# Routed tiles of a mixture-of-experts stage: gated rows turned by SyncE's transposing DMAs instead of TensorE, down product two tiles later

## The chip, the cores and the metric

The kernel runs on one core of one Trainium2 chip. The metric is the device time of one launch. Names used below: TensorE (PE, the matmuls; PEld its weight loads), VectorE (DVE), ScalarE (ACT), GpSimd (POOL) and SyncE (SP), which here only issues DMAs, in the order of its program. The core has 16 DMA engines; SP's transfers go over the hardware queue, POOL's accumulating ones over the software queue.

## The reference, cut to what matters

x has shape (8, 256, 512) in float32. A long convolution over products of value and context rows comes first and is added to x; the change doesn't touch it. Then follows the feed-forward part over T = 2048 tokens of 512 numbers:

```python
scores = sigmoid(xf @ gate_w.T)                    # 8 experts
topk_w, topk_idx = top_k(scores, 2)
topk_w = topk_w / (topk_w.sum(-1, keepdims=True) + 1e-20) * 2.5
shared_out = silu(xf @ shared_wg.T) * (xf @ shared_wu.T) @ shared_wd.T
h = silu(xf @ exp_wg[e].T) * (xf @ exp_wu[e].T)    # for each expert e, 352 wide
all_out = h @ exp_wd[e].T
out = x + shared_out + sum over the two picked experts of topk_w * all_out
```

## The kernel before

**Precision.** Every float32 operand of a product is split into a high and a low fp16 part, and a product is three fp16 matmuls, high x high, high x low and low x high (split_products, L734 to L736). So wherever a result becomes an operand, ScalarE makes the high part (a copy to fp16) and VectorE the low part (a subtraction).

**Routed tiles.** The pairs of token and expert are sorted by expert in a buffer in DRAM (pair_rows, fp16 high and low parts side by side), in tiles of 128 pairs. There are TILES = 39 places for tiles, as many as any routing can need. A tile that isn't needed is computed all the same, on rows that are thrown away. For every tile t:

- SyncE loads its rows with a transposing DMA (load_tile, L525, eight blocks of 128x128) into one of four slots (xg), and its token numbers and weights (load_ids, L528).
- tile_gate_up on TensorE: 24 matmuls of 352 columns, 12 for gate into bank 0 and 12 for up into bank 1. The transposed rows are the stationary operand, so the result has tokens on partitions.
- ScalarE: silu of the gate (tile_silu, L1147). VectorE: silu times up into hm (tile_gated, L1535).
- tile_hidden on TensorE: the down product needs the hidden numbers on partitions, so three 128x128 transposes in float32 turn hm into bank 3 (L930). The third overlaps the second, since 352 isn't a multiple of 128; its rows that come twice meet weights that are zero.
- ScalarE copies bank 3 to fp16 (tile_hidden_high, L1159), VectorE subtracts (tile_hidden_low, L1540), both into mixT (hgh, hgl).
- tile_down on TensorE: 9 matmuls of 512 columns into bank 4. ScalarE scales the result by the pair's weight (tile_out, L1154), and POOL adds it to the rows of out with an indirect accumulating DMA (add_tile, L697).

**Order around the change.** All orders are written out by hand, one program for each engine, with semaphores between them. TensorE's loop is gate/up of t, down of t-1, transposes of t. The add of tile t waits for the add of t-2; where t begins another expert, or is a tile not needed, it waits for t-1 as well (tile_prev), since a token can occur in both. SyncE loads the rows of t+4 when gate/up of t has left their slot, and the ids of t+4 when the add of t has landed. Tile 0 is interleaved with the last down product of the shared part.

**Expert weights.** They are loaded raw, four pieces an expert, into staging buffers, and turned into fp16 parts by ScalarE (L1068) and VectorE (L1398). Expert 7 comes last: SyncE loads it behind the store of the last group of base rows (L401, out of x_tok), and its conversion is queued on ScalarE and VectorE between the work of tiles 1 and 2 (two pieces each). TensorE waits for all weights before it enters its loop at tile 5.

Of the kernel before, what the change touches and what calls it, by code (L numbers as in the profile page):

```python
# [5 lines left out]
ALU = mybir.AluOpType  # L6
# [7 lines left out]
P = 128  # L14
# [24 lines left out]
TILES = 2 * T // P + E - 1  # L39
EROWS = T + P  # L40
# [13 lines left out]
def xattn_moe(nc, x, ctx, ctx_hidden, skip, krev, gate_w, shared_w, expert_w, consts, table0, zeros, out):  # L54
# [8 lines left out]
    with ExitStack() as stack:  # L63
# [132 lines left out]
        hgh, hgl = (mixT[:, EX_PIECE + i * FK * P // 2:EX_PIECE + (i + 1) * FK * P // 2].bitcast(F16) for i in range(2))  # L196
# [22 lines left out]
        rows_in = [sem(f"rows_in{i}") for i in range(RING)]  # L219
        added = [sem(f"added{i}") for i in range(2)]  # L220
# [160 lines left out]
        def _(sp):  # L381
# [162 lines left out]
            for t in range(RING, 2 * RING):  # L544
                sp.wait_ge(r_gu, t - RING + 1)
                load_tile(t, t % RING)
                if t >= RING + 2:
                    sp.wait_ge(added[t % 2], 16)
                    load_ids(t - 2, t - 2 - RING)
            with sp.Fori(2, TILES // RING) as j:  # L550
                for u in range(RING):
                    t = j * RING + u
                    sp.wait_ge(r_gu, t - RING + 1)
                    sp.sem_inc(sp_passed, 1)
                    load_tile(t, u)
                    sp.wait_ge(added[u % 2], 16 * (j * (RING // 2) + (u - 2 - RING) // 2 + 1))
                    sp.sem_inc(sp_passed, 1)
                    load_ids(t - 2, (u + 2) % RING)
            for t in range(TILES // RING * RING, TILES + 2):
                if t < TILES:  # L560
                    sp.wait_ge(r_gu, t - RING + 1)
                    load_tile(t, t % RING)
                sp.wait_ge(added[t % 2], 16 * ((t - 2 - RING) // 2 + 1))
                load_ids(t - 2, (t - 2) % RING)
# [154 lines left out]
        def _(pe):  # L719
# [206 lines left out]
            def tile_hidden(t):  # L926
                pe.wait_ge(r_hm, t + 1)
                for k in range(FK):
                    c = min(k * P, FF - P)
                    last = nc.tensor.transpose(bank[3][:, k * P:(k + 1) * P], hm[:, c:c + P], ident)  # L930
                last.then_inc(r_hT, 1)

            def tile_down(t, w):
                pe.wait_ge(r_hl, t + 1)
                if not isinstance(t, int) or t > 0:
                    pe.wait_ge(r_y, t)
                last = split_products(
                    bank[4],
                    lambda k: (hgh[:, k * P:(k + 1) * P], hgl[:, k * P:(k + 1) * P]),
# [10 lines left out]
            tile_hidden(0)  # L950
            for t in range(1, RING + 1):
# [3 lines left out]
                if t == 1:  # L955
                    pe.wait_ge(base_ready, Q * (G - 1) + 1)
                tile_down(t - 1, weights_of(t - 1))
                if t < RING:
                    following = weights_of(t + 1), need_of(t + 1)
                tile_hidden(t)  # L960
            pe.wait_ge(piece_l, (E - 1) * EX_PARTS)
            with pe.Fori(1, (TILES - 3) // RING) as j:
                for u in range(1, RING + 1):
                    t = RING * j + u
                    tile_gate_up(t, u % RING, j + u // RING + 1, weights_of(t))
                    tile_down(t - 1, weights_of(t - 1))
                    tile_hidden(t)
            for t in range(TILES - 2, TILES):
                tile_gate_up(t, t % RING, t // RING + 1, weights_of(t))
                tile_down(t - 1, weights_of(t - 1))  # L970
                tile_hidden(t)
            tile_down(TILES - 1, weights_of(TILES - 1))
# [3 lines left out]
        def _(act):  # L976
# [180 lines left out]
            def tile_hidden_high(t):  # L1157
                act.wait_ge(r_hT, t + 1)
                nc.scalar.copy(hgh, bank[3][:, 0:FK * P]).then_inc(r_hh, 1)  # L1159

            tile_silu(0)
            tile_hidden_high(0)
# [465 lines left out]
```

## Time and profile before

| | before |
|---|---|
| median of 3 runs | 769.8 us (769.48 to 770.99) |
| the profiled execution | 771.41 us |
| its span, first to last instruction | 769.6 us |
| mean granted TensorE clock | 0.96 |
| busy | PE 679.9 us (88%), DVE 434.9, POOL 387.1, ACT 288.2 |
| DMA | 84.28 MB, 110 GB/s on the mean |
| hardware queue, software queue | 33.5% and 13.7% of 16 engines' span |

Busy times are shares of the whole span, over stages with different limits. The routed tiles take the last third of it, from 517.5 us on. A matmul's listed duration (0.31 or 0.38 us) overlaps the next one's; how fast they follow is read from their starts. A wait is put down to the event that came last.

### The profile page before, as it was taken

The page shows a single profiled execution, that of the slowest core. Times are in us where ns is not written, and L with a number is a line of the kernel's source. Part 1 is how long each engine was busy: PE and PEld are TensorE (multiplying, and loading weights), DVE is VectorE, ACT ScalarE, POOL GpSimd, SP SyncE. Part 2 cuts the span into 40 slices and gives each one's busy share as a digit, 9 for nine tenths or more (in the row PEclk, how much of TensorE's full clock was granted, in tenths as well). Part 3 has the DMA queues.
Part 4 walks back from the last instruction along what each step waited for, and adds up shares of the span by engine and source line. Part 5 has one row for each costly group of instructions (what it writes and reads, how often), then busy time and mean ns, then how long its engine had stood idle before and what let it go on. Part 6 is the DMA issues. An engine that isn't in the chain of part 4 may idle for free.

```text
span 769.6 us, 11432 instructions
## 1 busy us (share of the span) xinstructions
PE 679.9 (88%) x3552; PEld 343.8 (45%) x3553; DVE 434.9 (57%) x662; ACT 288.2 (37%) x362; POOL 387.1 (50%) x333
## 2 busy tenths in 40 slices
PE   1786977969989969989999988798999999999992
PEld 1333433424444434444444433334566666665661
DVE  4798689667975666877695685872311111111110
ACT  4436646444223534223531257452322222222220
POOL 2889988385782574783867107700222322222231
PEclk9998998989999989999999999989899999999998
DMA  7933223601334600314224288986765565656533
GB/s 206 270 89 95 88 78 68 151 6 23 131 76 100 147 14 29 123 29 81 58 68 156 78 252 291 316 174 171 113 94 93 85 89 90 94 82 93 91 50 41
DMA packets 101364, 84.28 MB, mean 110 GB/s; under 512 B 68064, under 2 KB 81888, under 8 KB 100768
## 3 DMA queue, kind: packets, MB, share of 16 engines
q1 hardware_dynamic: 92128, 65.16, 33.5%
q0 software_dynamic: 9200, 18.65, 13.7%
q8 instruction: 21, 0.34, 0.2%
q14 instruction: 15, 0.12, 0.1%
HBM read 44.35 MB, written 25.68 MB: 91 GB/s over the span
## 4 chain that ended last, share of the span: by engine, by line
PE 59%; DVE 14%; ACT 9%; POOL 8%; issue 5%; DMA 3%; SPq 1%; POOLq 0%; another core or an unknown queue 0%; DVEq 0%; ACTq 0%
PE banks L734 18%; PE banks L736 18%; PE banks L735 18%; POOL arena L584 5%; POOL arena L609 2%; DVE stats L1243 2%; DVE arena L1230 2%; DVE mixT L1237 2%; PE banks L756 2%; PE banks L930 2%; ACT arena L1068 2%; DVE arena L1216 1%; DMA arena<-split_filters 1%; DVE hm L1364 1%; DMA stages<-in_expert_w 1%
## 5 line engine op out<-in xcount | busy, mean ns | idle before, releaser
L584 POOL TENSOR_TENSOR arena<-arena 128x512 f32<-128x512 f32 x124 | 136.1, 1129 | 67.0 <-DVE arena L1216 65.7
L697 POOL DMA_INDIRECT out<-xf,ids x39 | 60.8, 1559 | 198.8 <-ACT xf L1154 95.6
L734 PE MATMUL banks<-arena 128*128 128x512 f16 x320 | 125.3, 392 | 19.6 <-DVE arena L1230 9.7
L735 PE MATMUL banks<-arena 128*128 128x512 f16 x320 | 125.3, 392 | 0.6 <-issue 0.6
L736 PE MATMUL banks<-arena 128*128 128x512 f16 x320 | 125.1, 391 | 0.0
L1230 DVE TENSOR_TENSOR arena<-banks,arena 128x512 f32<-128x512 f32 x128 | 81.5, 683 | 38.3 <-PE banks L736 37.9
L734 PE MATMUL banks<-arena,normed 128*128 x312 | 98.4, 315 | 0.4 <-issue 0.4
L735 PE MATMUL banks<-arena,normed 128*128 x312 | 98.3, 315 | 0.0
L736 PE MATMUL banks<-arena,normed 128*128 x312 | 98.2, 315 | 0.0
L989 ACT ACTIVATE arena<-arena 128x2048 f16<-128x2048 f32 x31 | 59.1, 1907 | 87.3 <-POOL arena L584 87.2
L609 POOL TENSOR_TENSOR arena<-arena 128x512 f16<-128x512 f32 x68 | 78.8, 1191 | 7.6 <-ACT arena L989 7.5
L1540 DVE TENSOR_TENSOR mixT<-banks,mixT 128x384 f16<-128x384 f32 x39 | 21.8, 558 | 99.5 <-ACT mixT L1159 99.5
L1154 ACT ACTIVATE xf<-banks,ids 128x512 f32<-128x512 f32 x39 | 26.8, 687 | 126.9 <-PE banks L736 124.0
L1237 DVE TENSOR_REDUCE mixT<-arena 128x256 f32<-128x2048 f32 x32 | 73.1, 2285 | 1.0
L734 PE MATMUL banks<-xf,arena 128*128 128x512 f16 x176 | 68.8, 391 | 2.8 <-DVE hm L1364 2.4
L735 PE MATMUL banks<-xf,arena 128*128 128x512 f16 x176 | 68.8, 391 | 0.0
L736 PE MATMUL banks<-xf,arena 128*128 128x512 f16 x176 | 68.6, 390 | 0.0
L1535 DVE SCALAR_TENSOR_TENSOR hm<-banks,silu 128x352 f32<-128x352 f32 x39 | 20.5, 525 | 82.5 <-PE banks L736 82.5
L982 ACT ACTIVATE arena<-arena 128x1024 f16<-128x1024 f16 x32 | 33.7, 1054 | 84.4 <-PE banks L736 71.7
L734 PEld LDWEIGHTS banks<-arena 128*128 128x128 f16 x320 | 32.1, 100 | 62.5 <-issue 20.2
L735 PEld LDWEIGHTS banks<-arena 128*128 128x128 f16 x320 | 32.1, 100 | 40.4 <-issue 7.0
L736 PEld LDWEIGHTS banks<-arena 128*128 128x128 f16 x320 | 32.1, 100 | 40.1 <-issue 4.6
(164 smaller groups left out, 1132.3 us busy)
## 6 DMA issues: line engine op xcount, KB each, us to landing
arena<-split_filters SPq DMA_DIRECT2D x32, 256.0 KB
arena<-in_expert_w SPq DMA_DIRECT2D x12, 544.0 KB, 8.2
stages<-in_expert_w SPq DMA_DIRECT2D x10, 544.0 KB, 6.2
arena<-in_ctx_hidden SPq DMA_DIRECT2D x4, 1024.0 KB, 8.1
arena<-in_ctx SPq DMA_DIRECT2D x8, 512.0 KB, 6.5
x_tok<-in_x SPq DMA_DIRECT2D x6, 512.0 KB, 7.4
out<-x_tok SPq DMA_DIRECT2D x6, 512.0 KB, 5.4
x_tok<-in_expert_w SPq DMA_DIRECT2D x5, 544.0 KB
```

Source lines behind the costliest of these rows:

```text
L584: nc.gpsimd.tensor_tensor(kv[s % 2][:, lb * COLS:(lb + 1) * COLS].rearrange("p (b j i) -> p b j i", i=NH, j=NH), v[:, a, None, :].to_broad ...
L609: nc.gpsimd.tensor_tensor(kvl[s % SPLITS][:, c], kv[s % 2][:, c], kvh[s % SPLITS][:, c], ALU.subtract).then_inc(kvl_by_pool, 1)
L697: nc.gpsimd.indirect_dma_start(out=out, out_offset=bass.IndirectOffsetOnAxis(ap=ids[slot][:, 0:1], axis=0), in_=yg[slot], in_offset=None, ...
L734: nc.tensor.matmul(dst, wh, xh, start=(k == 0), stop=False)
L735: nc.tensor.matmul(dst, wh, xl, start=False, stop=False)
L736: last = nc.tensor.matmul(dst, wl, xh, start=False, stop=(k == n - 1))
L982: nc.scalar.activation(filt[s % 2].rearrange("p (t l) -> p t l", t=2), back, ACT.Copy).then_inc(filt_ready, 1)
L989: nc.scalar.activation(kvh[s % SPLITS], kv[s % 2], ACT.Copy).then_inc(kvh_ready, 1)
L1154: nc.scalar.activation(yg[slot], bank[4], ACT.Copy, scale=ids[slot][:, 1:2].bitcast(F32)).then_inc(r_y, 1)
L1230: nc.vector.tensor_tensor(prod[:, n * COLS:(n + 1) * COLS].rearrange("p (b j i) -> p b j i", i=NH, j=NH), bank[n].rearrange("p (b j i) -> ...
L1237: nc.vector.tensor_reduce(heads(mixT)[:, :, h * NH:(h + 1) * NH], prod.rearrange("p (a j i) -> p a j i", i=NH, j=NH), AX_X, ALU.add).then_ ...
L1540: nc.vector.tensor_tensor(hgl, bank[3][:, 0:FK * P], hgh, ALU.subtract).then_inc(r_hl, 1)
```

## The change

What turns the gated rows is moved from TensorE to the DMA engines, for all tiles but the last two:

- VectorE writes the gated rows into hm in two pieces: 256 columns, and the last 96 behind 32 columns of zeros. hm then has three whole blocks, and needs no overlap.
- ScalarE and VectorE split hm itself, token by token (tile_high, tile_low), into by_token, two slots in x_tok[1].
- SyncE turns both parts with one transposing DMA of six 128x128 blocks into by_hidden, two slots in mixT (turn_hidden), when the low part is there and the down product of t-2 has left the slot.
- TensorE's loop is gate/up of t, down of t-2. The down product waits for the DMA (hidden_in). gate/up of t waits for the gated rows of t-1 (r_hm), which the transposes did before.
- The last two tiles (TURNED_LAST) are transposed on TensorE as before, and both down products follow behind all else.
- On SyncE, expert 7's loads come right after the first ids, ahead of the store of the base rows, which now follows tile 0's turned rows. On ScalarE and VectorE its conversion comes at tiles 2 and 3 instead of 1 and 2.

The core of the diff:

```diff
+TURNED_LAST = 2
...
-        hgh, hgl = (mixT[:, EX_PIECE + i * FK * P // 2:EX_PIECE + (i + 1) * FK * P // 2].bitcast(F16) for i in range(2))
+        by_token, by_hidden = ([t[:, EX_PIECE + i * FK * P:EX_PIECE + (i + 1) * FK * P].bitcast(F16) for i in range(2)]
+                               for t in (x_tok[1].rearrange("p q l -> p (q l)"), mixT))
+        whole = (FK - 1) * P
+        hm_tail = slice(FK * P - FF + whole, FK * P)
...
-            sp.wait_ge(base_ready, Q * G)
-            store(out_rows[G - 1], x_tok[(G - 1) % 3], base_stored)
             load_expert(E - 1)
...
+            def turn_hidden(t, slot):
+                if not isinstance(t, int) or t >= 2:
+                    sp.wait_ge(r_down, t - 1)
...
+                sp.wait_ge(r_hl, t + 1)
...
+                sp.dma_start(by_hidden[slot].rearrange("p (a t) -> p a t", t=P), by_token[slot], transpose=True
+                             ).then_inc(hidden_in[slot], 16)
+
+            for t in range(RING):
+                sp.wait_ge(r_gu, t + 1)
+                load_tile(t + RING, t)
+                turn_hidden(t, t % 2)
+                if t == 0:
+                    sp.wait_ge(base_ready, Q * G)
+                    store(out_rows[G - 1], x_tok[(G - 1) % 3], base_stored)
+            with sp.Fori(1, TILES // RING - 1) as j:
                 for u in range(RING):
-                    t = j * RING + u
-                    sp.wait_ge(r_gu, t - RING + 1)
+                    t = RING * j + u
+                    sp.wait_ge(r_gu, t + 1)
                     sp.sem_inc(sp_passed, 1)
-                    load_tile(t, u)
...
+                    load_tile(t + RING, u)
+                    turn_hidden(t, u % 2)
+                    sp.wait_ge(added[u % 2], 16 * (RING // 2 * j + u // 2 - 1))
...
             def tile_gate_up(t, slot, n, w):
                 pe.wait_ge(rows_in[slot], 16 * n)
+                if not isinstance(t, int) or t > 0:
+                    pe.wait_ge(r_hm, t)
...
                 for u in range(1, RING + 1):
                     t = RING * j + u
                     tile_gate_up(t, u % RING, j + u // RING + 1, weights_of(t))
-                    tile_down(t - 1, weights_of(t - 1))
-                    tile_hidden(t)
-            for t in range(TILES - 2, TILES):
+                    tile_down(t - 2, u % 2, RING // 2 * j + u // 2, weights_of(t - 2))
+            for t in range(TILES - TURNED_LAST, TILES):
                 tile_gate_up(t, t % RING, t // RING + 1, weights_of(t))
-                tile_down(t - 1, weights_of(t - 1))
+                tile_down(t - 2, t % 2, t // 2, weights_of(t - 2))
                 tile_hidden(t)
-            tile_down(TILES - 1, weights_of(TILES - 1))
+            for t in range(TILES - TURNED_LAST, TILES):
+                tile_down(t, t % 2, None, weights_of(t))
...
+            def tile_high(t, slot, n):
+                act.wait_ge(r_hm, t + 1)
+                if not isinstance(n, int) or n > 0:
+                    act.wait_ge(hidden_in[slot], 16 * n)
+                nc.scalar.copy(by_token[slot][:, 0:FK * P], hm[:, 0:FK * P]).then_inc(r_hh, 1)
...
             for t in range(1, RING + 1):
                 tile_silu(t)
-                tile_out(t - 1, (t - 1) % RING, (t - 1) // RING + 1)
-                tile_hidden_high(t)
-
-                if t <= 2:
-                    expert(E - 1, *(first_half, second_half)[t - 1])
+                tile_high(t, t % 2, t // 2)
+                if t >= 2:
+                    tile_out(t - 2, (t - 2) % RING, (t - 2) // RING + 1)
+                if 2 <= t <= 3:
+                    expert(E - 1, *(first_half, second_half)[t - 2])
...
             def tile_gated(t):
+                if not isinstance(t, int) or t > 0:
+                    dve.wait_ge(r_hl, t)
...
+                nc.vector.scalar_tensor_tensor(out=hm[:, 0:whole], in0=bank[1][:, 0:whole], scalar=1 / WS,
+                                               in1=silu[:, 0:whole], op0=ALU.mult, op1=ALU.mult)
+                nc.vector.scalar_tensor_tensor(out=hm[:, hm_tail], in0=bank[1][:, whole:FF], scalar=1 / WS,
+                                               in1=silu[:, whole:FF], op0=ALU.mult, op1=ALU.mult).then_inc(r_hm, 1)
+
+            def tile_low(t, slot):
+                dve.wait_ge(r_hm, t + 1)
                 dve.wait_ge(r_hh, t + 1)
-                nc.vector.tensor_tensor(hgl, bank[3][:, 0:FK * P], hgh, ALU.subtract).then_inc(r_hl, 1)
-
+                nc.vector.tensor_tensor(by_token[slot][:, FK * P:2 * FK * P], hm[:, 0:FK * P],
+                                        by_token[slot][:, 0:FK * P], ALU.subtract).then_inc(r_hl, 1)
```

The order of instructions shows three places. The first is TensorE's loop, between the last matmul of one tile's down product (from mixT) and the first of the next tile's gate/up (from normed, the slot's rows); L930 are the transposes. Before:

```order
L736 MATMUL banks<-arena,mixT 128x512
L927 REGISTER_ALU
L930 MATMUL banks<-con,hm 128x128 [waits r_hm]
L930 MATMUL banks<-con,hm 128x128 x2
L896 ISA
L896 TENSOR_LOAD tile_w
L896 ISA x2
L734 ISA [waits rows_in3]
L734 MATMUL banks<-arena,normed 128x352
```

After:

```order
L755 MATMUL banks<-arena,mixT 128x512
L915 ISA
L915 TENSOR_LOAD tile_w
L915 ISA x2
L753 ISA [waits r_hm,rows_in3]
L753 MATMUL banks<-arena,normed 128x352
```

The two rows of transposes are gone, and the wait for hm stands at the gate/up instead. The second place is one tile of SyncE's loop. Before:

```order
L522 ISA [waits r_gu]
L522 TENSOR_LOAD tile_row
L522 ISA x2
L525 ISA
L525 DMA_TRANSPOSE normed<-pair_rows 128x8x128
L556 ISA
L522 TENSOR_LOAD tile_row [waits added0]
L522 ISA x2
L528 ISA
L528 DMA ids<-pair_table 128x2
```

After:

```order
L527 ISA [waits r_gu]
L527 TENSOR_LOAD tile_row
L527 ISA x2
L530 ISA
L530 DMA_TRANSPOSE normed<-pair_rows 128x8x128
L556 DMA_TRANSPOSE mixT<-x_tok 128x6x128 [waits r_down,r_hl]
L573 REGISTER_ALU
L527 ISA [waits added0]
L527 TENSOR_LOAD tile_row
L527 ISA x2
L533 ISA
L533 DMA ids<-pair_table 128x2
```

Between the load of a tile's rows and its ids there is now the DMA that turns the split rows, with two waits, and the waits of the ids stand behind it. The third place is SyncE at the start of the routed tiles, from the last of the first four ids on. Before:

```order
L522 TENSOR_LOAD tile_row
L522 ISA x2
L528 ISA
L528 DMA ids<-pair_table 128x2
L401 DMA out<-x_tok 64x4x512 [waits base_ready]
L401 DMA out<-x_tok 64x4x512
L417 DMA stages<-in_expert_w 128x1088 [waits piece_l] x2
L417 DMA x_tok<-in_expert_w 128x1088 [waits piece_l]
L417 DMA mixT<-in_expert_w 128x1088 [waits piece_l]
L522 TENSOR_LOAD tile_row [waits r_gu]
L522 ISA x2
L525 ISA
L525 DMA_TRANSPOSE normed<-pair_rows 128x8x128
```

After:

```order
L527 TENSOR_LOAD tile_row
L527 ISA x2
L533 ISA
L533 DMA ids<-pair_table 128x2
L422 DMA stages<-in_expert_w 128x1088 [waits piece_l] x2
L422 DMA x_tok<-in_expert_w 128x1088 [waits piece_l]
L422 DMA mixT<-in_expert_w 128x1088 [waits piece_l]
L527 TENSOR_LOAD tile_row [waits r_gu]
L527 ISA x2
L530 ISA
L530 DMA_TRANSPOSE normed<-pair_rows 128x8x128
L556 DMA_TRANSPOSE mixT<-x_tok 128x6x128 [waits r_hl]
L406 DMA out<-x_tok 64x4x512 [waits base_ready]
L406 DMA out<-x_tok 64x4x512
```

The store of the base rows (L401, now L406) has moved from ahead of expert 7's loads to behind the first turned rows.

## Rows read from the trace of the kernel before

**Rows 1.** Windows: us, busy time per engine, granted clock, DMA share, GB/s.

```profile
625.00:685.00 60.00, 60.00 (x372) 36.87 (x371) 11.39 (x21) 15.70 (x32) 16.41 (x11) 1.00 0.61 92
```

**Rows 2.** Timeline, one tile: start us, us, engine, line, operation, idle before.

```profile
639.32 0.38 PE L734 MATMUL banks<-arena,mixT 128*128 x1
...
639.52 0.53 DVE L1535 SCALAR_TENSOR_TENSOR hm<-banks,silu 128x352 f32<-128x352 f32 x1 [2.21 <-PE banks L736]
...
640.99 1.27 SPq L525 DMA_TRANSPOSE normed<-pair_rows  x1
...
641.26 0.49 PE L930 MATMUL banks<-con,hm 128*128 128x128 f32 x3
...
641.59 0.31 PE L734 MATMUL banks<-arena,normed 128*128 x1
...
642.18 0.47 ACT L1159 CAST mixT<-banks 128x384 f16<-128x384 f32 x1
...
642.69 0.56 DVE L1540 TENSOR_TENSOR mixT<-banks,mixT 128x384 f16<-128x384 f32 x1 [2.65 <-ACT mixT L1159]
...
643.08 0.35 SPq L528 DMA_DIRECT2D ids<-pair_table  x1
...
645.17 0.38 PE L734 MATMUL banks<-arena,mixT 128*128 x1
```

**Rows 3.** Windows, 538 to 540 us.

```profile
538.00:540.00 2.00, 0.45 (x2) 0.45 (x3) 1.50 (x2) 0.67 (x2) 0.00 (x0) 0.50 1.14 238
```

**Rows 4.** Timeline, start of the routed stage.

```profile
525.87 3.16 SPq L401 DMA_DIRECT2D out<-x_tok  x2
...
529.07 2.52 SPq L417 DMA_DIRECT2D stages<-in_expert_w  x2
...
532.13 0.43 SPq L417 DMA_DIRECT2D mixT<-in_expert_w  x1
...
533.29 9.48 SPq L525 DMA_TRANSPOSE normed<-pair_rows  x3
...
534.54 0.38 PE L736 MATMUL banks<-arena,mixT 128*128 x1
...
536.63 1.11 ACT L1068 ACTIVATE arena<-stages 128x1088 f16<-128x1088 f32 x1 [0.69 <-DMA stages<-in_expert_w]
...
538.98 0.52 DVE L1535 SCALAR_TENSOR_TENSOR hm<-banks,silu 128x352 f32<-128x352 f32 x1
539.55 0.90 PE L930 MATMUL banks<-con,hm 128*128 128x128 f32 x3 [4.64 <-DVE hm L1535]
...
545.72 0.38 PE L734 MATMUL banks<-arena,mixT 128*128 x1
```

**Rows 5.** Timeline and chain of waits (start us, us, what), the end.

```profile
754.88 1.55 POOL L697 DMA_INDIRECT out<-xf,ids  x1 [4.23 <-ACT xf L1154]
...
760.40 1.56 POOL L697 DMA_INDIRECT out<-xf,ids  x1 [3.97 <-DMA out<-xf,ids]
...
754.88 4.65 DMA out<-xf,ids
```

**Rows 6.** Timeline, SyncE ahead of the routed stage.

```profile
510.96 4.82 SPq L525 DMA_TRANSPOSE normed<-pair_rows  x2
516.89 3.79 SPq L528 DMA_DIRECT2D ids<-pair_table  x4
```

**Rows 7.** Transposing DMAs at L431: durations in ns, landing in us.

```profile
L431 SPq DMA_TRANSPOSE xf<-stages x8: 1232/1272/1368, 126.8 to 239.9; - x8
...
DMA to landing us min/median/max: 3.1/3.2/3.8
```

**Rows 8.** DMA queues and issues, 600 to 760 us.

```profile
q1 hardware_dynamic: 27888, 6.06, 19.9%
...
normed<-pair_rows SPq DMA_TRANSPOSE x23
```

**Rows 9.** Landing of the adds, L697.

```profile
DMA to landing us min/median/max: 4.6/4.8/9.2
```

More of the change, by code:

```diff
@@ L219, in xattn_moe @@
         rows_in = [sem(f"rows_in{i}") for i in range(RING)]
+        hidden_in = [sem(f"hidden_in{i}") for i in range(2)]
         added = [sem(f"added{i}") for i in range(2)]
@@ L540, in _ @@
                 load_ids(t, t)
-            sp.wait_ge(base_ready, Q * G)
-            store(out_rows[G - 1], x_tok[(G - 1) % 3], base_stored)
             load_expert(E - 1)
-            for t in range(RING, 2 * RING):
-                sp.wait_ge(r_gu, t - RING + 1)
[L546 to L550, printed above, removed]
+            def turn_hidden(t, slot):
+                if not isinstance(t, int) or t >= 2:
+                    sp.wait_ge(r_down, t - 1)
+                    if not isinstance(t, int):
+                        sp.sem_inc(sp_passed, 1)
+                sp.wait_ge(r_hl, t + 1)
+                if not isinstance(t, int):
+                    sp.sem_inc(sp_passed, 1)
+                sp.dma_start(by_hidden[slot].rearrange("p (a t) -> p a t", t=P), by_token[slot], transpose=True
+                             ).then_inc(hidden_in[slot], 16)
@@ L554, in _ @@
                     sp.sem_inc(sp_passed, 1)
[L555 to L556 removed]
+                    load_tile(t + RING, u)
+                    turn_hidden(t, u % 2)
+                    sp.wait_ge(added[u % 2], 16 * (RING // 2 * j + u // 2 - 1))
                     sp.sem_inc(sp_passed, 1)
[L558 to L564, printed above, removed]
+                    load_ids(t, u)
@@ L566, in _ @@
+            for t in range(TILES // RING * RING - RING, TILES):
+                if t + RING < TILES:
+                    sp.wait_ge(r_gu, t + 1)
+                    load_tile(t + RING, t % RING)
+                if t < TILES - TURNED_LAST:
+                    turn_hidden(t, t % 2)
+                sp.wait_ge(added[t % 2], 16 * (t // 2 - 1))
+                load_ids(t, t % RING)
             sp.wait_ge(base_stored, 32 * G)
@@ L1544, in _ @@
             add_shared(G - 1, 2)
             add_shared(G - 1, 3)
-            for t in range(1, 3):
+            for t in range(1, RING + 1):
                 tile_gated(t)
-                tile_hidden_low(t)
-                expert(E - 1, *(first_half, second_half)[t - 1])
-            with dve.Fori(1, (TILES - 3) // 2) as j:
+                tile_low(t, t % 2)
+                if 2 <= t <= 3:
+                    expert(E - 1, *(first_half, second_half)[t - 2])
+            with dve.Fori(RING // 2, (TILES - 3) // 2) as j:
@@ L1553, in _ @@
                     tile_gated(t)
-                    tile_hidden_low(t)
-            for t in range(TILES - 2, TILES):
+                    tile_low(t, u % 2)
+            for t in range(TILES - TURNED_LAST, TILES):
                 tile_gated(t)
-                tile_hidden_low(t)
+                tile_turned_low(t, t % 2)
 def constants():
```

56 lines of the change are left out of this document (31 added, 25 removed).

## The prediction

> **What bounds the kernel now.** I read the page first, then a table of windows over the routed tiles, one tile of the timeline, and the timeline and the chain of waits at the two ends of that stage. From 625 to 685 us TensorE is busy all the time at full clock, with the DMA engines at a share of 0.61 [rows 1]. So in the loop nothing but TensorE's own instructions sets the pace, 5.85 us a tile, and the reader can take that apart [rows 2]: the 24 gate/up matmuls run from 641.59 to 645.17 (3.58 us), the 9 matmuls of a down product from 639.32 to 641.26 (1.94), and three transposes from 641.26 to the next gate/up at 641.59 (0.33). At both ends the stage isn't bound by TensorE. At its start TensorE has nothing from 534.54 + 0.22 to 539.55 and comes back at a granted clock of 0.50, the 1.2 GHz level [rows 3, 4]. At its end the chain runs over two accumulating DMAs, one after the landing of the other [rows 5].
>
> **Part 1, the transposes leave TensorE.** 39 tiles had three each; the last two keep them. Of these 39, I compare up to the last matmul of the down product that ends the pipeline (37 before, 36 after, below), and there 37 of 38 groups are gone: 37 x 0.33 = **-12.2 us**. In the loop a tile should take 5.85 - 0.33 = 5.52 us.
>
> What has to be hidden for that. After a gate/up ends at E, VectorE starts 0.20 later (639.32 to 639.52) [rows 2]. It now runs two pieces. Its 352 columns take 0.53 us and its 384 columns 0.56 [rows 2], so about 1 ns a column and 0.17 fixed, and pieces of 256 and 96 columns cost 0.43 + 0.27 = 0.70. Then come ScalarE's copy, 0.47, and VectorE's subtraction, 0.56 [rows 2]; each now reads SBUF and not PSUM, which I leave at the same price. With 0.1 between them the low part is there at about E + 2.3. SyncE first reads a row number and issues the next tile's load: that DMA starts 1.67 after the gate/up's end and holds SyncE 1.27 (639.32, 640.99) [rows 2], so the new transpose is issued at about E + 3.0. By then its second condition, down(t-2) complete at E + 1.94, holds as well. A transposing DMA of eight 128x128 blocks from SBUF lands 3.1 to 3.8 us after its issue [rows 7]; at worst it also waits for the tile load before it, another 3.8. So it lands between E + 6 and E + 11. It is wanted at E + 1.94 + 3.58 + 1.94 + 3.58 = E + 11.0. The cover is 5 us by the middle value and about nothing at the worst. I take it as hidden.
>
> Of the wider road: the share of the DMA engines was 0.61 over 5.85 us, 3.6 us of all sixteen a tile. The hardware queue took 19.9% of 160 us for 23 loads, 1.4 us each [rows 8]; three quarters of that more is 1.0, and 3.6 + 1.0 = 4.6 in 5.52 us is a share of 0.83. That fits, with less air. The SP queue's round is 1.27 (load), 0.82 to the next issue, 0.35 (ids) (642.26, 643.08) [rows 2] and now up to 1.27 more, with again 0.82 before the load when it doesn't sleep: 4.5 us, under 5.52.
>
> TensorE gets a new wait before gate/up(t), for the gated rows of t-1. They are there at E + 0.95, while a down product (1.94) lies between: nothing in the loop. Where no down product lies between, at t = 2, it costs 0.20 + 0.70 + 0.05 = **+0.95 us** (0.05 is what TensorE took after VectorE, 538.98 + 0.52 to 539.55 in rows 4).
>
> **Part 2, the start of the routed stage.** SyncE stood at the base rows of the last group until 525.87, stored them, and only from 529.07 loaded expert 7 [rows 4]. ScalarE got its second piece at 536.63, and the gated rows of tile 2, queued on VectorE behind the low part of that piece, came at 538.98. TensorE stood for them. Without it, down(2) would have begun at 534.76 + 0.33 + 3.58 = 538.67; it began at 545.72. That is **-7.05 us** (4.79 of idling, 2.3 of slow clock and late start). The change issues these loads straight after the ids, which end at 516.89 + 3.79 = 520.7 [rows 6], lets the store follow, and takes the conversion of expert 7 one tile later, so the data should be in by about 530, before ScalarE asks at about 534.
>
> What is late next: the first two new transposes, which stand behind these loads on SyncE. Four pieces take 3.5 us to issue (529.07 to 532.56) [rows 4], so load(4) is issued at about 525. When down(0) wants its rows: gate/up(2) began at 534.76 - 1.94 - 3.58 = 529.24; a down product and two groups of transposes go from before it, 0.95 comes, so 527.6, and 3.58 later it is 531.2. Lower end: transposes at 1.27 each, landing in time, no stall. Upper end, from the row at 533.29 (three transposes behind such a load held SyncE for 9.48 us, 3.2 each): load(4) and turn(0) end at 531.4, landing 1.9 later (3.2 less the 1.27 of the issue) at 533.3, which is 2.1 late. Then the store (3.2), load(5) and turn(1) at 3.2 each, landing at 542.9 against 538.8: 4.1 more, and 2.3 for a slow clock. Middle: after the loads of expert 6 two transposes took 4.82 us [rows 6]; that gives turn(0) at 525.2 + 4.8 + 1.9 = 531.9 (0.7 late), and turn(1), behind a store of 3.2 and two issues at 1.6 and 1.27, at 538.0 plus the same bulk's delay of about 1.3, against 537.4 (1.9 late): **+2.6 us**. I take the middle, since those rows are the same situation (load, then transposes, no store ahead); the ends are 0 and 8.5.
>
> **Part 3, the end.** Let X be the end of the down product right behind the last gate/up. Before it was down(37), and add(37) started at 754.88, add(38) at 760.40, only after add(37) had landed (4.65 us) plus 0.87 [rows 5]; the kernel ended 9.2 later. Now it is down(36). Two adds follow, and I take each to wait for the landing before it, as add(38) did: the pace is 5.52 each. That is one more, **+5.52**, while one down product less lies before X, **-1.94**. The two down products and their copies (1.94 + 0.25 + 0.69 each) run inside that chain. A lower end: add(37) doesn't wait for add(36), then it starts at X + 5.0 and not X + 7.4, 2.4 us less.
>
> **Sum** against the profiled execution (771.41 us, span 769.6): -12.2 + 0.95 - 7.05 + 2.6 + 5.52 - 1.94 = -12.1, so 759.3. The median of the runs was 1.6 lower, 769.8, so **757.7 us**.
>
> **Rivals.**
> A. *The first transposes are very late* (upper end of part 2): 8.5 in place of 2.6, 763.6 us. For it speaks the 9.48 row; against it that a store of 1 MB stood ahead of the loads there.
> B. *The start's stall stays.* If expert 7's conversion, one tile later, holds the gated rows of tile 3 as it held those of tile 2, the 7.05 isn't won and hides the other late things (0.95 + 2.6): 757.7 + 7.05 - 3.55 = 761.2. Against it: ScalarE waited for the DMA there [rows 4], and now that comes 8 us earlier.
> C. *Transposes pass one at a time.* The eight-block one lands in 3.2 [rows 7], six blocks would be 2.4, together 5.6 a tile against 5.52: 37 x 0.08 = +3.0, 760.7. If the adds land later for it, only those that wait for the add before them feel it. The Trainium skill ("VectorE: DVE Perf Modes", section "The three transpose paths") gives 1309 ns for one 128x128 block by the DMA crossbar and 390 ns on TensorE, and advises TensorE where the result may lie in PSUM. Read as a price per block, fourteen blocks would be 18.3 us a tile and the kernel several hundred us slower; the trace disagrees, since eight blocks land in 3.1 to 3.8 us, and TensorE's three cost 0.33 here.
> D. *SyncE becomes the bound, and the kernel is slower.* Place: its round per tile. If each of its three issues pays the long way of the load, the round is 1.67 + 1.27 + 0.82 + 1.27 + 0.82 + 0.35 = 6.2 us. The loss against 5.52 is 37 x 0.68 = 25 us: 783. It decides from a round of 5.85, where the 12.1 are eaten up. For it: 1.67 from the gate/up's end to the issue [rows 2]. Against it: that interval holds a wake-up too, which a SyncE that is late doesn't pay; between load and ids it was 0.82.
>
> The Trainium skill ("DMA: Bandwidth & Descriptors", section "Queues, rings and completion order") says that each DMA engine takes turns between the queues it has work for, packet by packet. By that the adds, on the other queue, land later beside more transposes; the trace has 4.6 to 4.9 us beside one transpose a tile and 4.65 alone [rows 5, 9], so hardly any of it shows, and the sum by that rule would stay.
>
> **Chances.** Forecast 0.62, A 0.13, B 0.08, C 0.08, D 0.06, and 0.03 that gains and losses cancel. This kernel's measurement can't tell less than 0.2% (1.5 us) from no change. A, B, C and nearly all of the forecast lie below 768.3, so faster 0.90, same 0.03, slower 0.07. The forecast's own range is 754 (no late transpose, the lower end of part 3) to 762; to hold 8 in 10 it has to take in B, C and most of A: 753 to 765.
>
> **What would show it.** In the loop, gate/up starts 5.52 us apart with TensorE never waiting for a DMA; the SyncE row of the new transpose about 3 us behind a gate/up's end; expert 7's loads issued at about 521 and no idle of 4 us on TensorE near 535; a wait of about 1 us before gate/up(2) and waits of 1 to 2 us for the transposes ahead of down(0) and down(1); two adds at a distance of 5.5 us behind the end of down(36). It would be wrong if TensorE waits for the transposed rows in the loop, if the distance of the adds grows past 5.85 throughout, or if SyncE's loads creep later from tile to tile.

## The result, and the profile after

The changed kernel takes **759.4 us** (757.6 to 762.2, four runs) beside 769.6 us of the kernel before on the same chip (four runs): a ratio of 0.987, interval 0.984 to 0.990. Forecast were 757.7 us and 753 to 765.

The profiled execution took 757.6 us, its span is 755.8, and the granted clock over it 0.957. The second row below has the window of [rows 1]. The columns are busy time of TensorE, its weight loads, VectorE, ScalarE and GpSimd, then granted clock, DMA share and GB/s.

```profile
565.00:625.00 60.00, 60.00 (x360) 35.03 (x359) 12.62 (x33) 18.29 (x33) 16.94 (x12) 1.00 0.79 127
625.00:685.00 60.00, 60.00 (x360) 35.03 (x359) 12.62 (x33) 17.86 (x33) 16.68 (x11) 1.00 0.82 131
```

TensorE is still busy all the time at the full clock. The DMA engines rose from 0.61 to about 0.8. One tile in the timeline, beside [rows 2]:

```profile
598.53 0.38 PE L753 MATMUL banks<-arena,mixT 128*128 x1
...
598.73 0.42 DVE L1568 SCALAR_TENSOR_TENSOR hm<-banks,silu 128x256 f32<-128x256 f32 x1 [3.65 <-PE banks L755]
599.07 0.25 DVE L1570 SCALAR_TENSOR_TENSOR hm<-banks,silu 128x96 f32<-128x96 f32 x1
599.43 0.51 ACT L1185 CAST x_tok<-hm 128x384 f16<-128x384 f32 x1 [2.02 <-DVE hm L1570]
...
600.04 0.56 DVE L1576 TENSOR_TENSOR x_tok<-hm,x_tok 128x384 f16<-128x384 f32 x1 [0.72 <-ACT x_tok L1185]
...
601.00 1.26 SPq L530 DMA_TRANSPOSE normed<-pair_rows  x1
602.45 1.23 SPq L556 DMA_TRANSPOSE mixT<-x_tok  x1
...
602.45 1.56 POOL L716 DMA_INDIRECT out<-xf,ids  x1 [3.98 <-DMA out<-xf,ids]
...
604.99 0.36 SPq L533 DMA_DIRECT2D ids<-pair_table  x1
...
606.43 1.26 SPq L530 DMA_TRANSPOSE normed<-pair_rows  x1
```

The low part is there 2.1 us after the gate/up's end (598.53 to 600.60), the new transpose is issued 3.9 after it (602.45), and the gated rows of the next tiles come 5.52 us apart. SyncE's round, from one tile load to the next, is 606.43 - 601.00 = 5.43 us here, but other rounds of the same trace take up to 5.83: the 23 rounds between the loads at 567.80 and 695.15 take 5.54 each on the mean. That is TensorE's 5.52 and a little more, so nothing was spare. The loads do creep: they are issued 2.4 us behind a gate/up's end at 567.80 and 2.7 to 3.1 behind it around 690.

The start of the routed stage, beside [rows 4]:

```profile
519.42 0.91 SPq L422 DMA_DIRECT2D stages<-in_expert_w  x2
...
521.98 1.81 SPq L530 DMA_TRANSPOSE normed<-pair_rows  x1
523.83 1.91 SPq L556 DMA_TRANSPOSE mixT<-x_tok  x1
...
525.65 0.32 PE L753 MATMUL banks<-arena,normed 128*128 x1 [0.93 <-DVE hm L1570]
532.09 0.39 PE L753 MATMUL banks<-arena,mixT 128*128 x1 [2.69 <-issue]
```

Expert 7's loads go out at 519.4 in place of 529.1, and the 4.64 us of idling are gone. In their place stand 0.93 ahead of gate/up(2) and 2.69 ahead of down(0). The end, from the timeline and the chain of waits, beside [rows 5]:

```profile
733.78 0.70 ACT xf L1178
735.46 4.79 DMA out<-xf,ids
741.12 4.67 DMA out<-xf,ids
746.45 1.78 POOLq L64
...
746.67 1.56 POOL L716 DMA_INDIRECT out<-xf,ids  x1 [3.99 <-DMA out<-xf,ids]
```

Two adds now wait, each for the landing of the one before it, where there was one. For the add at 741.12 the scaled rows had been there since 736.92 + 0.69 = 737.61, while the add before it landed at 735.46 + 4.79 = 740.25.

To see which part gave what, I cut the routed stage of every trace into three: *start* (begin of gate/up(0) to tile 3's gated rows), *loop* (34 tiles, to tile 37's gated rows) and *end* (to the end of the span). In us:

| kernel | start | loop | end | sum | ratio of the times to before (interval) |
|---|---|---|---|---|---|
| before | 28.4 | 199.5 | 24.2 | 252.1 | 1 |
| after | 23.0 | 187.4 | 30.0 | 240.4 | 0.987 (0.984 to 0.990) |
| c0_after | 23.1 | 190.0 | 30.0 | 243.1 | 0.988 (0.985 to 0.991) |
| e1_before_early_load | 22.0 | 198.8 | 24.1 | 244.9 | 0.992 (0.989 to 0.995) |
| e2_after_late_load | 31.7 | 188.2 | 29.6 | 249.4 | 0.997 (0.995 to 0.999) |
| e3_tail_order | 22.6 | 187.4 | 29.5 | 239.5 | 0.984 (0.980 to 0.987) |
| e4_no_last_add | 22.7 | 189.3 | 24.2 | 236.2 | 0.979 (0.976 to 0.983) |
| e5_turn_first | 22.7 | 190.7 | 30.2 | 243.7 | 0.986 (0.983 to 0.989) |
| e6_two_turns | 22.4 | 224.7 | 29.5 | 276.6 | 1.035 (1.032 to 1.037) |
| e7_lag_one | 27.2 | 201.1 | 24.2 | 252.5 | 1.004 (1.001 to 1.006) |
| e8_ids_on_act | 22.5 | 187.4 | 30.0 | 239.9 | 0.987 (0.984 to 0.990) |
| e9_ids_two_turns | 22.9 | 189.3 | 30.3 | 242.6 | 0.987 (0.983 to 0.990) |
| e11_early_wait | 23.1 | 190.0 | 29.5 | 242.6 | one run |
| e10_all | 22.9 | 187.5 | 28.9 | 239.2 | 0.985 (0.983 to 0.987) |

The stage before this one scatters too: gate/up(0) began at 517.5 before and at 515.5 after, 2.1 us that no edit touches. So of the two profiled runs' 13.8 us the change holds 11.7.

### The profile page after: what moved, and what is told of

Read it like the earlier page. It is cut to its first block, busy times and chain, and to the rows that moved or that the text cites. A ratio compares the mean times of both kernels' runs of the same rounds, so it can differ in the third digit from the quotient of the medians.

```text
span 755.8 us, 11521 instructions
## 1 busy us (share of the span) xinstructions
PE 663.5 (88%) x3441; PEld 329.3 (44%) x3442; DVE 438.5 (58%) x702; ACT 292.9 (39%) x362; POOL 387.2 (51%) x333
## 4 chain that ended last, share of the span: by engine, by line
PE 61%; DVE 14%; ACT 8%; POOL 7%; DMA 4%; issue 4%; SPq 1%; POOLq 0%; DVEq 0%; ACTq 0%
PE banks L753 20%; PE banks L754 19%; PE banks L755 19%; POOL arena L603 4%; PE banks L775 2%; DVE stats L1274 2%; DMA arena<-split_filters 2%; POOL arena L628 2%; DVE mixT L1268 1%; DVE arena L1261 1%; DMA out<-xf,ids 1%; ACT arena L1092 1%; DVE arena L1247 1%; DVE hm L1395 1%; DVE arena L1429 1%
## 5 line engine op out<-in xcount | busy, mean ns | idle before, releaser
L1568 DVE SCALAR_TENSOR_TENSOR hm<-banks,silu 128x256 f32<-128x256 f32 x39 | 16.5, 424 | 130.8 <-PE banks L755 120.0
L753 PE MATMUL banks<-arena,mixT 128*128 x117 | 44.4, 379 | 4.4 <-issue 2.7
L1185 ACT CAST x_tok<-hm 128x384 f16<-128x384 f32 x37 | 18.9, 511 | 73.5 <-DVE hm L1570 71.5
```

Of the source, the lines that this page charges most:

```text
L753: nc.tensor.matmul(dst, wh, xh, start=(k == 0), stop=False)
L1185: nc.scalar.copy(by_token[slot][:, 0:FK * P], hm[:, 0:FK * P]).then_inc(r_hh, 1)
L1568: nc.vector.scalar_tensor_tensor(out=hm[:, 0:whole], in0=bank[1][:, 0:whole], scalar=1 / WS, in1=silu[:, 0:whole], op0=ALU.mult, op1=ALU.mult)
```

## The experiments

They ran on three chips: c0 to e3 where the kernel before takes 770.3 us, e4 to e7 where it takes 769.4, and e8 to e11 where it takes 763.8. So ratios are compared, not times, and differences in us are made from ratios.

**c0_after: the changed kernel again,** as the control that the others are compared with.

> The changed kernel once more, so that the variants on this chip have their neighbour. Theory T: three terms, each by itself: 37 groups of transposes gone from TensorE (-12.2 us), expert 7's loads ahead of the store (-7.0, given back in part by 1 us before gate/up(2) and 2.8 us for the first turned rows), one more add in the chain behind the last gate/up (+5.6 less a down product of 1.9). Together -10 to -12 us against the kernel before, so 758 to 760. Rival R: the gain comes from the moved loads alone and the transposes were hidden anyway; the same total, but then the next run must show nearly all of it.

761.0 us, ratio 0.988. Its profile has the same start and end; the loop is 2.6 us longer, in six intervals of 5.7 to 6.2 us.

This trace also shows how close SyncE is. Its rounds take 5.68 us on the mean (565 to 700 us), and its loads are issued 3.9 to 5.6 us behind a gate/up's end from 571 to 707. The chain of waits of this run doesn't go over TensorE there but over SyncE's queue alone, from 545 to 690 us, and ends in a wait of TensorE for turned rows (two rows of the chain, then TensorE's row):

```profile
690.15 1.26 SPq L530
691.61 4.51 DMA mixT<-x_tok
```

```profile
696.24 0.39 PE L753 MATMUL banks<-arena,mixT 128*128 x1 [0.23 <-DMA mixT<-x_tok]
```

So in the same kernel SyncE can be the bound of the loop, and what it cost in this run is at most the 2.6 us.

**e1_before_early_load: part 2 alone, in the kernel before.**

```diff
+            load_expert(E - 1)
             sp.wait_ge(base_ready, Q * G)
             store(out_rows[G - 1], x_tok[(G - 1) % 3], base_stored)
-            load_expert(E - 1)
```

> The kernel before, with one edit: SyncE loads expert 7 ahead of the store of the base rows. T: TensorE's wait of 4.6 us at 535 and the slow clock behind it go, -5 to -7 us, 763 to 765, and the loop stays at 5.85 us a tile. R: -10 us or more, as in the changed kernel. Third possibility: the store, now behind the loads, holds the first adds so long that the tiles wait for them, and the gain is under 2 us.

764.2 us beside 770.3, ratio 0.992: 6.3 us gained, all of it in the start (-6.4). The loop keeps its 5.85. More than half of the gain of the whole change has nothing to do with the transposes.

**e2_after_late_load: the changed kernel with the loads back behind the store.**

```diff
+            sp.wait_ge(base_ready, Q * G)
+            store(out_rows[G - 1], x_tok[(G - 1) % 3], base_stored)
             load_expert(E - 1)
...
                 turn_hidden(t, t % 2)
-                if t == 0:
-                    sp.wait_ge(base_ready, Q * G)
-                    store(out_rows[G - 1], x_tok[(G - 1) % 3], base_stored)
```

> The changed kernel, with expert 7's loads put back behind the store. T: the first turned rows now come behind store and loads; load(4) is issued at about 531, turn(0) some 3 us later and lands at 540 or so, where down(0) wants it at 529 of that trace: TensorE stands for about 10 us and gets a slow clock, so 8 to 13 us slower than the changed kernel, 767 to 772, about what the kernel before takes; the loop stays at 5.5. R: all of the gain is gone, 769 to 770. The two differ in the loop's period, which the trace shows.

767.1 us, ratio 0.997: without the early load a gain of 0.3% is left. The loop has its 5.52, but TensorE's row ahead of down(0) is

```profile
537.28 0.60 PE L752 MATMUL banks<-arena,mixT 128*128 x1 [9.41 <-DMA mixT<-x_tok]
```

That is rival A's case: turned rows behind a store and an expert's loads in SyncE's queue. The start costs 31.7 us, more than the 28.4 of the kernel before. What the loop wins, the start and the end nearly eat up without the early load.

**e4_no_last_add: the end.** The changed kernel without tile 38's add (its product is left out of the result).

```diff
-            for t in range(TILES - 2, TILES):
+            for t in range(TILES - 2, TILES - 1):
                 add_tile(t, t % RING, 16 * (t // 2), before_of(t))
```

> The changed kernel without the add of tile 38 (its product is computed, but left out of the result). T: the end is a chain of adds at a distance of 5.5 us, so 5.5 us faster than the changed kernel. S (TensorE's order sets the end): the last add that is left is that of tile 37, which would follow its own product, and TensorE's last down product hides behind it: about 3 us faster.

753.5 us, ratio 0.979 beside the control's 0.988, so 6.7 us. The end falls from 30.0 to 24.2 us, by 5.8. A last add costs about the distance of two adds (5.55 and 5.66 in the changed kernel).

**e3_tail_order: the down products of tiles 36 and 37 each brought forward behind the next gate/up,** so that their adds could begin earlier.

```diff
+                if t < TILES - 1:
+                    tile_down(t - 2, t % 2, t // 2, weights_of(t - 2))
+                    tile_hidden(t)
+                    tile_down(t - 1, (t - 1) % 2, (t + 1) // 2, weights_of(t - 1))
+                else:
+                    tile_down(t - 1, (t - 1) % 2, None, weights_of(t - 1))
+                    tile_hidden(t)
```

> The changed kernel with another order at the end: down(36) right after gate/up(37), down(37) right after gate/up(38), so that only one down product is left behind, as in the kernel before. T (the end is set by the chain of adds, each of tiles 36 to 38 waiting 5.5 us for the landing before it): at most 0.4 us faster, since the chain starts from add(35) in both. Rival S (the end is set by TensorE's order, the number of down products behind the last gate/up): 3.6 to 5 us faster.

757.5 us, ratio 0.984 (0.980 to 0.987) beside 0.988 (0.985 to 0.991): better by 3.3 us on the mean, but the intervals overlap, and the profiles give it 0.5 in the end. They also say why it can't be more. Rows of its chain of waits (start us, us, what):

```profile
723.81 4.50 DMA out<-xf,ids
...
729.17 4.67 DMA out<-xf,ids
...
734.78 4.79 DMA out<-xf,ids
...
740.45 4.43 DMA out<-xf,ids
```

Each add in this chain lands in 4.2 to 4.9 us and the next is issued about 0.9 later. The last eight adds start at 707.19 to 745.75, 5.51 apart on the mean and 5.2 to 5.9 singly, as their landings vary. For the last tiles, where an add waits for the one right before it, the adds are a chain with a pace of their own, about the same as TensorE's 5.52. Work that is ready earlier finds the adds in front of it.

**e5_turn_first: turn(0) ahead of expert 7's loads, turn(1) ahead of the load of tile 5.** It asks whether the 2.69 us are late turned rows.

```diff
+            turn_hidden(0, 0)
+            load_expert(E - 1)
+            sp.wait_ge(base_ready, Q * G)
+            store(out_rows[G - 1], x_tok[(G - 1) % 3], base_stored)
+            sp.wait_ge(r_gu, 1)
+            load_tile(RING, 0)
+            turn_hidden(1, 1)
```

> The changed kernel with SyncE's start reordered: turned rows of tile 0 ahead of expert 7's loads, those of tile 1 ahead of the rows of tile 5. T: the 2.7 us that TensorE waits ahead of down(0) is the landing behind the bulk of the loads and goes: 2 to 3 us faster, 756 to 757. Rival U: the loads come 1.5 us later and the store stands in front, so the wait moves to down(1) or to expert 7's conversion: no change.

759.1 us, ratio 0.986, 1.5 us better on the mean, within the intervals. turn(0) is issued 2.7 us earlier, but TensorE still waits 2.43 us and down(0) still begins at 531.92. The theory falls, or the rows were held up elsewhere.

**e11_early_wait: e5, and TensorE waits for turned rows 0 ahead of gate/up(2).**

```diff
+                if t == 2:
+                    pe.wait_ge(hidden_in[0], 16)
```

> The start with turn(0) ahead of expert 7's loads, and TensorE's wait for turned rows 0 put ahead of gate/up(2) instead of ahead of down(0). It separates what the 2.4 to 2.7 us ahead of down(0), labelled as issue and not as a wait, are. Theory R (turned rows 0 are late, landing at about 532): gate/up(2) starts at about 532 instead of 525.7, with a PE row there that names the DMA, and down(0) follows without a gap: routed stage 6 us longer less 2.4. Theory I (they have landed by about 525 and the gap is TensorE's instruction supply behind the bulk of the weight loads): gate/up(2) starts within 0.5 us of 525.7 and the gap of about 2.4 us ahead of down(0) stays, or moves with the instruction queue's packet at 528 to 531.

It separates the two. SyncE's transpose and TensorE's two rows:

```profile
516.77 1.28 SPq L554 DMA_TRANSPOSE mixT<-x_tok  x1
...
521.37 0.32 PE L757 MATMUL banks<-arena,normed 128*128 x1 [0.93 <-DVE hm L1576]
...
527.97 0.39 PE L757 MATMUL banks<-arena,mixT 128*128 x1 [2.71 <-issue]
```

gate/up(2) starts with the usual 0.93 behind VectorE, so the turned rows had landed by 521.4. Ahead of down(0), 6.6 us later, the 2.71 us of idling are there all the same. In this run rows that are late don't cause them. In the ten traces with this gap the profile puts it down to the turned rows in six (c0, e3, e4, e6, e8, e9) and to "issue" in four (the changed kernel's first, e5, e10, e11). For the six no run puts the wait elsewhere, so a late landing isn't excluded there; but the gap is of the same size, and it came in e11 without one.

**e6_two_turns: every tile of the loop issues a second transposing DMA of six blocks,** extra work that nothing waits for but SyncE.

```diff
+                    sp.wait_ge(spare_in, 16 * t - 16 * RING)
+                    sp.sem_inc(sp_passed, 1)
+                    sp.dma_start(hTh.rearrange("p m c -> p (m c)")[:, 0:2 * FK * P].rearrange("p (a t) -> p a t", t=P),
+                                 hTl.rearrange("p m c -> p (m c)")[:, TG:TG + 2 * FK * P], transpose=True).then_inc(spare_in, 16)
```

> The changed kernel with a second transposing DMA of the same size (six blocks, from and to buffers that nobody uses then) behind each turn in the loop, for 28 tiles: what the cover is worth. If SyncE's round (about 4.5 us of work by the trace, now 5.8) or the DMA engines (share 0.8, now about 0.97) set the pace from here, 28 tiles take 0.2 to 0.6 us more each: 5 to 17 us slower. If both have room left: no change.

795.6 us, +35. SyncE's rows in the timeline, then what TensorE waited for from 545 to 770 (us in total, times, longest) and the window 565 to 725:

```profile
601.34 1.27 SPq L531 DMA_TRANSPOSE normed<-pair_rows  x1
602.88 1.21 SPq L557 DMA_TRANSPOSE mixT<-x_tok  x1
604.29 1.21 SPq L562 DMA_TRANSPOSE hTh<-hTl  x1
606.82 0.37 SPq L534 DMA_DIRECT2D ids<-pair_table  x1
608.23 1.28 SPq L531 DMA_TRANSPOSE normed<-pair_rows  x1
```

```profile
PE banks L760 <- DMA mixT<-x_tok: 26.9, 27, 1.8
```

```profile
565.00:725.00 160.00, 133.57 (x764) 73.24 (x762) 26.95 (x71) 36.84 (x70) 36.32 (x24) 1.00 0.80 132
```

SyncE's round is 6.89 us. The two wide gaps in it are where row numbers are read: the load and the ids each need a number in a register first, and 604.29 + 1.21 to 606.82 is 1.3 us, 607.19 to 608.23 is 1.0. The DMA share is 0.80, as in the changed kernel, while TensorE does a sixth less in the same time.

**e9_ids_two_turns: e6, with the loads of row numbers taken from SyncE to ScalarE's queue.** If SyncE's round is the bound and not the transfers, the 35 us go.

```diff
+            def load_ids(t, slot, n):
+                act.wait_ge(added[slot % 2], 16 * n)
+                r = act.value_load(tile_row[0:1, bass.ds(t, 1)], min_val=0, max_val=TROWS - P)
+                act.dma_start(ids[slot][:], table[bass.ds(r, P), :]).then_inc(ids_in[slot], 16)
```

> Does extra work: the second transposing DMA per tile of the run with two turns, and the row numbers' loads on ScalarE's queue instead of SyncE's. With two turns the round of SyncE was 6.9 us and the period about 7.0 (795.6 us). Theory D (SyncE's issuing is what bounded that run): the round falls by 0.36 + 1.1 to 1.3 = about 1.5 us to 5.4, so the period returns to 5.5 to 5.6 and the time to 761 to 767 us. Theory E (the DMA engines or the transposes' passage bounded it): the period stays at 6.5 to 7.0 and the time at 785 to 796 us.

754.6 us, ratio 0.987, the same as without the second transpose. SyncE's rows and the same window:

```profile
599.80 1.24 SPq L531 DMA_TRANSPOSE normed<-pair_rows  x1
601.23 1.36 SPq L557 DMA_TRANSPOSE mixT<-x_tok  x1
602.78 1.23 SPq L562 DMA_TRANSPOSE hTh<-hTl  x1
605.25 1.24 SPq L531 DMA_TRANSPOSE normed<-pair_rows  x1
```

```profile
565.00:725.00 160.00, 159.16 (x947) 92.02 (x945) 32.72 (x86) 47.04 (x85) 45.17 (x29) 1.00 0.92 157
```

The round is 5.45 us (5.4 to 6.4 in the loop) and the loop 189.3. At a DMA share of 0.92 TensorE is still busy 159.16 of 160 us. It was SyncE's issuing that cost the 35 us, and twenty blocks a tile pass beside everything else, where the changed kernel has fourteen.

**e7_lag_one: the down product one gate/up stage later, and not two.**

```diff
                     tile_gate_up(t, u % RING, j + u // RING + 1, weights_of(t))
-                    tile_down(t - 2, u % 2, RING // 2 * j + u // 2, weights_of(t - 2))
+                    tile_down(t - 1, (u - 1) % 2, RING // 2 * j + (u + 1) // 2, weights_of(t - 1))
```

> The changed kernel with the down product one gate/up stage later and not two: gate/up(t), down(t-1). T: the turned rows land 6 to 8 us behind a gate/up's end and are now wanted at 5.5, so TensorE waits 1 to 2.5 us in each of 37 tiles: 35 to 95 us slower. Rival V: the second stage of delay buys nothing, the rows are there in time: the same time or 5 us faster, since the end is one product shorter.

771.6 us, ratio 1.004, some 12 us over the control: neither number. The end is 5.8 us shorter (one add less behind the last gate/up), the start 4.2 longer, the loop 13.7. Its intervals are 5.91 us on the mean and scatter from 5.5 to 6.9, and TensorE waits from 520 to 760:

```profile
PE banks L753 <- DMA mixT<-x_tok: 10.6, 13, 4.3
```

With one stage of lag the turned rows are wanted 5.5 us after their gate/up's end. Where TensorE waited for them in the loop (from 575 us on) it started again 5.8 to 6.4 us after that end, 2.9 to 3.6 us after SyncE's issue. That is the low end of the 6 to 8 that I expected, and so the waits there are 0.2 to 0.4 us in some of the tiles and not 1 to 2.5 in each.

**e8_ids_on_act: the changed kernel with the row numbers' loads on ScalarE's queue.** The edit is that of e9, without the second transpose; SyncE's work in a round falls by the 0.36 and one read, to an estimated 3.9 us of the 5.54.

> The loads of the adds' row numbers (36 of them, from tile 4 on) go from SyncE's queue to ScalarE's, issued there ahead of the tile's copy. SyncE's round per tile falls from about 5.43 us (1.26 load, 0.19, 1.23 turn, 1.31 to the row numbers, 0.36, 1.08 to the next load) to about 1.26 + 1.23 + one row number read of 1.1 to 1.3, 3.8 us. Theory L (the kernel after is just short of being bound by SyncE, and the loops' scattered intervals of 5.7 to 6.2 us in the control's profile come from a SyncE that is late): the steady intervals stay 5.52 us and the long ones vanish, up to 2.6 us, so 758 to 760 us where the control had 761. Theory I (the long intervals come from elsewhere, TensorE's own instruction supply for one, since the idle ahead of them isn't put down to a wait): 761 and the same scatter. If ScalarE's extra issue of about 1.3 us a tile were to delay its copies of the gated rows' low part: intervals above 5.52 throughout, slower by 37 times the excess.

752.8 us beside 763.8, ratio 0.987 against the control's 0.988: no difference that can be told. Its profile shows no long interval in the loop (187.4). But the first one of the changed kernel, e2 and e3 have none behind the first tiles either, with all of SyncE's work in the round; c0, e4, e5, e9 and e11 have some, up to 6.44. Two clean traces of two with a short round (this and e10) and three of eight with a long one.

How late SyncE is parts the traces more sharply. Between the issue of a tile's turned rows and its down product lie, from 570 us on, never less than 8.2 us in e8 and e10 and never less than 6.5 in the changed kernel's first, e2 and e3; in the five with long intervals the least is 4.0 to 4.6. In four of those five SyncE had fallen behind before the first long interval, in e4 only after it. That a late SyncE makes the intervals long is likely by this, but not shown: TensorE's rows ahead of them say "issue", and only c0's chain goes over SyncE.

**e10_all: e3, e5's start and e8 together.**

> Three edits together: down(36) and down(37) each behind the gate/up that follows them (the tail order, 757.5 us measured), turn(0) and turn(1) ahead of the loads behind which they stood (759.1 measured), and the row numbers' loads on ScalarE's queue. Taking the measured ratios to the kernel before, 0.9836 and 0.9859 against the control's 0.9879: if the gains add, -3.3 and -1.5 us from the control, and -0 to -2.6 for the row numbers, 754 to 757 us. If the row numbers on ScalarE cost something or the start's gap isn't the turned rows, 757 to 760.

752.5 us, ratio 0.985 (0.983 to 0.987) against 0.987 for e8 on the same chip and 0.988 for the control: the gains don't add to the 754 to 757 that were forecast for a chip at 770 (0.979 to 0.983). Its end is 28.9 us, with the adds still a chain, from 686.91 on, and 2.47 us ahead of down(0) remain. It is as fast as any kernel here that does the whole work, but not shown to beat the changed one.

## Why the prediction was right, point by point

- **Part 1, the loop: right.** Forecast 5.52 us a tile, measured 5.52 (the 34 tiles in 187.4 us, before in 199.5, of which 0.6 is one long interval). Right, too, in this trace, that TensorE never waits for the turned rows there; c0 has one wait of 0.23 us. The cover was worked out wrong: the middle of "between E + 6 and E + 11" is 8.5, which leaves 2.5 us and not 5. From 575 us on the changed kernel issues the turned rows 6.5 to 7.5 us ahead of their down product, later than the E + 3.0 of the prediction (E + 3.5 to 4.5). With e7's 2.9 to 3.6 us from issue to use an estimate of the cover is 2.9 to 4.7 us, and in c0, where an issue stood 4.4 us ahead, at most 1.5.
- **The wait before gate/up(2): right,** 0.95 forecast, 0.93 measured.
- **The ramp stall of 7.05: right, 0.7 too large.** The 4.64 us of idling are gone, and e1 alone gives 6.3 to 6.4. Rival B is out.
- **"+2.6 for the late first turns": the size fits, the cause doesn't.** It had 0.7 ahead of down(0) and 1.9 ahead of down(1). Measured are 2.69 ahead of down(0) and nothing ahead of down(1). e11 shows the same gap with rows that had landed at least 6.6 us before. The true lateness there is unknown, and the number came out by luck. Rival A isn't the changed kernel's case, but it is e2's.
- **The end: right.** A second add in the chain, forecast +5.52, in e4 5.8, in e7 5.8. The lower end, an add(37) that doesn't wait, didn't happen: 735.46 to 741.12 is 5.66.
- **The sum: -12.1 forecast, -11.7 measured** from gate/up(0) on. The 13.8 of the two spans hold 2.1 from ahead of it, and the medians give 10.3. The closeness is partly luck: sorted into the stretches of the table the prediction has -8.3 for the start, -9.3 for the loop and +5.5 for the end, where -5.4, -12.1 and +5.8 were measured. The start gave 2.9 less (2.0 of it ahead of down(0)), and the loop 2.8 more, since the wait of 1.9 ahead of down(1) didn't come and the kernel before had its long interval there.
- **SyncE's round, "4.5 us, under 5.52": mis-sized.** It is 5.54 on the mean. The step took two gaps of 0.82; in the round of 5.43 shown above there are three, 1.31 before the ids, 1.08 before the load and 0.19 before the transpose. The prediction's sign of being wrong, loads that creep later from tile to tile, is there weakly in the first trace and plainly in c0. Rival D, put at 0.06 with 6.2 us, had no margin left against it: in c0 it cost up to 2.6 us, and e6 shows what lies behind, 35 us for one more issue. The chance was too low.
- **The DMA share: 0.83 forecast, 0.79 to 0.82 measured.** Rival C (transposes one at a time) is out by e9, whose three transposing DMAs a tile would take 3.2 + 2.4 + 2.4 = 8.0 us by its prices, where the measured loop has 189.3 / 34 = 5.57. The Trainium skill ("VectorE: DVE Perf Modes", section "The three transpose paths") gives 1309 ns for one 128x128 block by the DMA. Read as a price per block, an estimate by it is 26 us a tile for e9's twenty blocks; the trace, with its 5.57, disagrees.

What stays open is the 2.1 to 2.8 us ahead of down(0) (2.11 at the least, in e6). They are in all ten traces of a kernel with a lag of two and the early load, whatever stood ahead of the turned rows. TensorE also waits there for VectorE's base rows, but in the changed kernel these were done at 522.23, 7 us before. Two candidates are left. One instruction packet (0.02 MB) passes the DMA queues between 1.4 us before and 1.5 after the gap's begin, in each of these traces, beside loads that move some 400 GB/s at their height. The kernel before has its packet too, but with nothing beside it (0 GB/s); e1 has it between 526 and 527 beside 382 GB/s, and no gap. And TensorE's sequencer reads three numbers from SBUF there, behind a wait; but behind gate/up(3) there are as many, and no gap. Neither was tried. The intervals of 5.7 to 6.4 us in some loops have the same label ("issue", 0.2 to 0.7 us ahead of a gate/up) and are as open.

## What to carry to other kernels

Moving work from a full engine to DMAs is paid in the issuing queue: add up that queue's round with every register read, not only the issues, and compare it with the new period and not with the old. Look at what stands ahead of the first of the new transfers, for here the gain hung on an expert's loads being issued 10 us earlier. And when an engine's round is cut, list the others': TensorE is now at 5.52 us a tile, SyncE at 5.54 and the chain of adds in the last tiles at 5.51, and from 560 to 740 us 31 of 32 adds start behind a landing of a DMA, where 11 of 31 did before. By these numbers a further cut on any one of them alone gives little; only the one on SyncE was tried (e8), and it gave nothing that can be told.

## What the runs showed of the hardware

- Where SyncE reads a row number into a register between two issues, they lie 1.0 to 1.3 us apart in the rows above (1.08 and 1.31), with a semaphore wait that has long been met. On ScalarE the same read hides: in e8 the copy ends at 601.33 and the issue is there at 601.39.

```profile
600.64 0.69 ACT L1173 ACTIVATE xf<-banks,ids 128x512 f32<-128x512 f32 x1 [0.86 <-PE banks L750]
...
601.39 0.39 ACTq L1179 DMA_DIRECT2D ids<-pair_table  x1
```

- A transposing DMA of six blocks holds SyncE 1.2 us, as long as one of eight [rows 7]. Beside bulk loads such issues took 2.95 us (six blocks, e11 at 527.02) and 4.74 (eight, at 522.23).
- In e9 the DMA engines were busy 0.92 of the time with a loss on TensorE of 0.5% (159.16 of 160 us busy).
